# A graph network's edge-maximum passes: the strips' low halves move to VectorE, and every fourth edge block instead of every fifth is fetched by matrix products

## The reference: a four-layer graph network on 3125 nodes and 50000 edges

```
def _sage_pool_layer(x, src, dst, Wp, bp, Ws, Wn, b, n_nodes):
    m = jax.nn.relu(x @ Wp + bp)
    msgs = m[src]
    agg = jax.ops.segment_max(msgs, dst, num_segments=n_nodes)
    agg = jnp.where(jnp.isfinite(agg), agg, 0.0)
    return x @ Ws + agg @ Wn + b
```

```
gathered = support[edge_col] * edge_val[:, None]
out = jax.ops.segment_sum(gathered, edge_row, num_segments=x.shape[0])
```

## Time and profile before

| | us |
|---|---|
| median of 3 timed runs | 2809.11 (2801.65 to 2812.7) |
| the profiled execution, device time | 2804.64 |
| its span, first to last instruction | 2802.9 |
| first pass, window 663 to 1186 | 523 |
| second pass, window 1246 to 1771 | 525 |
| everything before, between and after the passes | 1754.9 |

### The profile page before, as it was taken

How to read it: one execution, slowest core, us unless ns; L and a number is a source line. 1 busy time by engine, 2 the same in 40 slices (tenths; PEclk the granted TensorE clock), 3 DMA queues, 4 the chain that set the end, 5 groups by cost and what they waited for, 6 DMA issues and landing times. The chain is left out here.

```text
span 2802.9 us, 72099 instructions
## 1 busy us (share of the span) xinstructions
PE 2456.9 (88%) x29232; PEld 1982.7 (71%) x29232; DVE 1763.4 (63%) x4833; ACT 1156.4 (41%) x2585; POOL 1299.8 (46%) x1607
## 2 busy tenths in 40 slices
PE   6998999986879888677889887469899999999999
PEld 3666777764556555445556655369899999999998
DVE  6997999986778877446768776320444444444444
ACT  5997888874434444424434444310311111111110
POOL 4007999974888888558888887410000000000000
PEclk8558999997999999789989998569999999999999
DMA  5103000013555555534545555549200000000000
GB/s 165 42 2 102 12 13 13 13 50 97 143 124 141 137 131 135 126 96 122 130 117 150 128 137 143 146 161 348 84 2 2 1 2 2 2 2 2 2 2 19
DMA packets 147170, 227.40 MB, mean 81 GB/s; under 512 B 55568, under 2 KB 112619, under 8 KB 146162
## 3 DMA queue, kind: packets, MB, share of 16 engines
q1 hardware_dynamic: 120350, 184.69, 22.0%
q0 software_dynamic: 22944, 36.72, 6.7%
q10 hardware_dynamic: 3540, 1.30, 0.2%
HBM read 122.26 MB, written 100.35 MB: 79 GB/s over the span
## 5 line engine op out<-in xcount | busy, mean ns | idle before, releaser
L1892 POOL DMA_INDIRECT max_row<-table,max_src_rows x640 | 670.5, 1048 | 181.7 <-issue 165.9
L1934 PE MATMUL max_far<-adj 128*96 128x512 f16 x1800 | 538.6, 401 | 7.7 <-issue 5.8
L2060 DVE TENSOR_SCALAR adj<-adj,node_numbers 128x512 f16<-128x512 f16 x900 | 325.0, 370 | 210.8 <-PE max_far L1934 129.2
L1758 POOL TENSOR_SCALAR e<-e 128x512 f32<-128x512 f32 (+1 forms) x625 | 365.7, 604 | 178.5 <-ACT e L1746 160.9
L2405 PE MATMUL prop<-g,adj 128*128 128x192 f16 x4608 | 387.2, 247 | 8.5 <-DVE g L2479 8.5
L1772 DVE TENSOR_TENSOR e<-e,a_ps 128x1024 f32<-128x1024 f32 (+1 forms) x313 | 372.3, 1195 | 32.6 <-PE a_ps L1684 12.6
L2405 PEld LDWEIGHTS prop<-g,adj 128*128 128x128 f16 x4608 | 380.7, 98 | 13.4 <-issue 9.2
L2405 PE MATMUL prop<-weights_then_states,adj 128*128 128x192 f16 x4608 | 384.3, 246 | 0.0
L2405 PEld LDWEIGHTS prop<-weights_then_states,adj 128*128 128x128 f16 x4608 | 378.9, 98 | 3.7 <-issue 2.5
L1746 ACT ACTIVATE e<-s_ps 128x512 f32<-128x512 f32 (+1 forms) x625 | 335.5, 585 | 60.2 <-PE o_ps L1696 37.8
L2513 DVE SCALAR_TENSOR_TENSOR support_parts<-prop,coef,weights_then_states 128x96 f32<-128x96 f32 x384 | 120.6, 314 | 303.9 <-PE prop L2405 226.0
(11 more groups left out here) (292 smaller groups left out, 3702.5 us busy)
## 6 DMA issues: line engine op xcount, KB each, us to landing
weights_then_states<-weights SPq DMA_DIRECT2D x100, 400.0 KB, 4.8
weights<-max_rows_w SPq DMA_DIRECT2D x52, 400.0 KB
rows_dram<-max_out SPq DMA_DIRECT2D x100, 192.0 KB
weights<-adj SPq DMA_DIRECT2D x48, 400.0 KB
max_same<-same_dram SPq DMA_DIRECT2D x196, 96.0 KB
rows_dram<-adj SPq DMA_DIRECT2D x96, 192.0 KB
max_row<-table,max_src_rows POOLq DMA_INDIRECT x640
adj<-ids_dram SPq DMA_DIRECT2D x36, 128.0 KB
```

Source lines behind the costliest of these rows:

```text
L1758: nc.gpsimd.tensor_scalar(e_tile(u), e_tile(u), math.exp(10.0), math.exp(-10.0), ALU.min, ALU.max).then_inc(clipped, 1)
L1892: nc.gpsimd.indirect_dma_start(row[i % RING][:, j, :], None, table_dram, bass.IndirectOffsetOnAxis(ap=src_rows[:, 4 * n + j:4 * n + j + 1] ...
L1934: mm = nc.tensor.matmul(far_ps[j % 2][0:D, :], parts[:, k, a, :], hot[(T * j + k) % HOTS], start=k == a == 0, stop=k == T - 1 and a == 1)
L2060: nc.vector.tensor_scalar(hot[i % HOTS], ids[j % 2], numbers[:, k:k + 1], None, ALU.is_equal).then_inc(hot_made, 1)
```

## The change

Two things change in `max_pass`, in both passes. The set of far blocks becomes every fourth block instead of every fifth: 22 instead of 18 blocks in a pass, with the first at block 4 instead of 5 and the last at block 88 instead of 90. And the low half of a strip is made by one VectorE instruction, which reads the sum in PSUM and the high half in SBUF and writes their difference. The product `take_high`, its semaphore, and ScalarE's `low_part` are gone. VectorE's new instruction stands right behind the scan in each step.

```
-FAR = range(5, 92, 5)
+FAR = range(4, 92, 4)
...
-            def take_high(n):
-
-                pe.wait_ge(hi_kept, n + 1)
-                nc.tensor.matmul(step_sums(n), minus[:, :], strip_at(0, n),
-                                 start=False, stop=True, skip_group_check=True).then_inc(hi_taken, 1)
...
-                if 1 <= m <= PARTS:
-                    take_high(m - 1)
...
+            def low_part(n):
+                dve.wait_ge(hi_kept, n + 1)
+                nc.vector.tensor_tensor(strip_at(1, n), by_source(n), strip_at(0, n), ALU.subtract).then_inc(lo_kept, 1)
...
                 if m >= SCAN:
                     scan(m - SCAN)
+                if 1 <= m <= PARTS:
+                    low_part(m - 1)
                 far(0, 1)
...
-            def low_part(n):
-                act.wait_ge(hi_taken, n + 1)
-                nc.scalar.activation(strip_at(1, n), by_source(n), ACT.Copy).then_inc(lo_kept, 1)
...
-                if 1 <= m <= PARTS:
-                    low_part(m - 1)
```

More of the change, by code:

```diff
@@ L1841, in max_pass @@
         piece_ps = ctx.enter_context(nc.psum_tensor(f"{name}_piece", [P, 1024], F16))
-        hots_ready, hots_used, hi_kept, hi_taken, lo_kept, piece_turned, piece_kept = (
-            sem("hots_ready"), sem("hots_used"), sem("hi_kept"), sem("hi_taken"), sem("lo_kept"),
+        hots_ready, hots_used, hi_kept, lo_kept, piece_turned, piece_kept = (
+            sem("hots_ready"), sem("hots_used"), sem("hi_kept"), sem("lo_kept"),
             sem("piece_turned"), sem("piece_kept"))
```

## The result

The changed kernel takes 2780.64 us (median of 5 runs, 2774.99 to 2786.23) against 2809.11 before (5 runs). The ratio is 0.9909, 95% interval 0.9890 to 0.9929: 0.9% faster. Its profiled execution took 2784.01 us, against 2804.64. The forecast was 2826 and its range began at 2783; the direction was wrong.

The account below looks back on a forecast made before the run. GpSimd was taken to set the 523 us pass; after the change VectorE's 528 us with 3 of waits gave 531, +8 in each pass, +16 on the profiled 2804.6, so 2826 us timed, range 2783 to 2866.

Parts of the forecast that it names:

- What bounds the kernel: In both passes GpSimd's transfers, issue gaps, first_key and tail sum to the whole 523 us, so GpSimd sets the pace.
- GpSimd's part: 16 fewer transfers save 21.2 us a pass; longer instructions beside a dense VectorE could eat it: 502 to 522 us.
- VectorE's part: Far comparisons add 29.7 us and the subtraction 50, raising VectorE's work from 380 to 459.5 us a pass.
- How full can it get?: VectorE's densest stretches, 0.92 and 0.89, taken as its limit; at 0.89 a pass takes 528 us, at 0.92 512.
- TensorE's part: Far products add 46 us, dropped work takes off 18 and 3; net +25 busy, needing 507 to 527 us a pass.
- The new wait: VectorE's low_part waits for ScalarE's high half of the strip: 3 us a pass, from bounds of 0 and 50.
- The sum: The slowest of three nearly equal engines plus losses between them: 531 us a pass, +8 in each, 2826 us timed.
- Rival 1: The saving survives: VectorE reaches 0.92, GpSimd keeps its durations; 512 us a pass, 2787 us; chance 0.22.
- the rule of the Trainium skill: GpSimd contends with VectorE's two-port or two-SBUF-input instructions; the subtraction, with one PSUM input, would slow no transfer.
- signs listed: If right: VectorE's share 0.87 to 0.90, its TensorE wait well under 67.4 us, subtraction about 0.57, transfers near 1.08 us.
- The one that decides: GpSimd would newly wait for TensorE to free row buffers, 10 us or more a pass against 1.1 before.
- wait of TensorE for far comparisons: This wait of TensorE on VectorE's comparisons was to appear if the forecast was right; no size given.

Follow-up runs that it names:

- e3: Changed kernel with GpSimd's first_key comparing 5 columns of 125 after the first four, output left stale: 2741.12 us, ratio 0.9773 of the kernel before.
- e9: Kernel before with first_key made by ScalarE and every fourth block far, low halves still by TensorE and ScalarE: 2660.10 us, ratio 0.9495.
- e2: Kernel before with only the low halves moved to VectorE's subtraction, every fifth block still far: 2810.42 us, ratio 1.0028.
- e1: Kernel before with only every fourth block far, low halves still by TensorE and ScalarE: 2777.66 us, ratio 0.9912.
- e10: Changed kernel with four buffers for the far comparisons instead of six: 2798.22 us, ratio 0.9983 of the kernel before.
- e4: Changed kernel with every third block far, subtraction on VectorE: 2790.21 us, ratio 0.9960 of the kernel before.
- e5: Changed kernel with first_key made by ScalarE instead of GpSimd, every fourth block far: 2672.15 us, ratio 0.9542 of the kernel before.
- e8: Kernel before with only first_key moved to ScalarE, every fifth block far, low halves by TensorE and ScalarE: 2667.36 us, ratio 0.9515.
- e12: Kernel before with first_key on ScalarE, every fourth block far, even strips' low halves by VectorE, odd by TensorE and ScalarE: 2665.08 us, ratio 0.9501.
- e6: Changed kernel with first_key made by ScalarE and every fifth block far, subtraction on VectorE: 2685.47 us, ratio 0.9589 of the kernel before.

## Why the prediction was wrong, point by point

**What bounds the kernel: right.** GpSimd's sum plus its tail was the pass before and after, and in e3 the pass fell with that sum. The forecast then handed the pass over to the other engines, and that was the error.

**GpSimd's part: right in kind.** The saving of 21.2 us was priced with durations between those of the pass and those of a dense stretch, 502 to 522 us. It came out at 511, in the middle. The longer instructions took 7 us back through the transfers (304 x 0.024) and 5 through `first_key`; a tail of 10.6 us in place of 13.4 gave 3. The text named this term and then let the others override it.

**VectorE's part: the work right, the ceiling wrong.** By the earlier trace rows the subtraction was put at 545 ns for 375 columns and 649 for 475, 571 on the mean; it measured 519 and 625, 546 on the mean. The work was put at 459.5 us and measured 454.9. The first step that failed is "How full can it get?". It read the shares 0.89 and 0.92 in the densest stretches of the earlier trace rows as VectorE's ceiling, and so had a pass of 528 us. In the changed kernel VectorE runs at 0.91 over a whole pass without the tail and at 0.96 between 850 and 950 us, and with every third block far at 0.99. With 0.985 in that formula the pass would have been (459.5 - 2.6)/0.985 + 14 = 478 us, well under GpSimd's 511.

**TensorE's part: wrong too, and by as much.** The text took the 502 us that were left after the wait for fetched rows (523 - 21.3) as TensorE's own need, and came to 507 to 527. That need was never so high. e9 gives TensorE all the work of the changed kernel and `take_high` on top, and its pass takes 450.5 us (at a granted clock of 0.97 against 0.94). The idle time that the trace of before gave to "issue" was counted as TensorE's own. The added work was mis-sized as well: +25 us busy was forecast, +13 measured. The product taken away was near (-18 forecast, -14.5 in e2). The four more far blocks were not: +43 forecast, +27 in e1, where the clock was 0.93 against 0.92. That makes about 0.15 us of busy time for each far product in place of 0.23; why, no run shows. So VectorE's ceiling alone would not have saved the forecast: with 478 for VectorE the largest upper end is TensorE's 527, and the same sum still gives no gain, some 2817 us. Both steps took what an engine does under GpSimd's pace for what it can do.

**The new wait: small, as forecast, but not of the forecast's kind.** 3 us a pass were forecast, as small losses in many steps. The row has 7.2 us, in four waits of 1.6 to 1.9 us, at 695 us and at 1134, 1152 and 1158, and none in the dense middle. It cost no time that shows: e2, with 8.9 us of it, has a pass as long as before (523.1 against 523).

**The sum.** It took the largest of three upper ends and added 3 us, on the ground that three nearly full engines lose time to each other. GpSimd lost 0.2 us to TensorE. That the row buffers between the two took up the rest is likely but not shown. In e10 a shorter ring did cost time, so the thought may have something in it; with six buffers it did not decide.

**The rivals.** Rival 1 (GpSimd keeps its saving, 2787 us) is what happened, within 7 us, at a chance of 0.22. But part of that is luck: it was priced by VectorE at a share of 0.92, 512 us, which happens to fall on GpSimd's own 511; and GpSimd did not keep its durations. By the rule of the Trainium skill beside it, GpSimd would stand near the lower end of 502 to 522 us; it stood in the middle. Of the signs listed, VectorE's share (0.91), its smaller wait (16.3 us) and the transfers (1.070) were near. The one that decides, GpSimd waiting 10 us or more for row buffers, went the other way (0.2 us), and no notable wait of TensorE for far comparisons appeared (2.3 us).

## What to carry to other kernels

When one engine's own instructions and issue gaps add up to the stage and nobody ever stops it, price the change on that engine first, and let another engine take over only when its work exceeds that sum. A busy share seen under that engine's pace is not a ceiling of the others, and the time left after subtracting their visible waits is not their need. Check the pace-maker by cutting its work alone (e3), for a closed sum is no proof where the others are full too (e4). Where a change has two parts, ask of each alone whether it touches the pace-maker: here one did and gained 0.9%, the other did not and gained nothing. Then look at what else stands on the pace-maker and could be made elsewhere: two ScalarE instructions in place of one of GpSimd's were worth four times the change that was studied.

## What the runs showed of the hardware that was not expected

VectorE can be busy for 0.99 of 500 us with waits in its order of work, and TensorE at the same time (e4).

GpSimd's transfers are longer in the midst of a pass than at its end. The last transfers of the first pass, when VectorE has almost nothing left to do, take 0.94 us in the kernel before, the changed kernel, e4, e5 and e9 alike. The mean over a pass went from 1.02 us (e8) to 1.20 (e4, VectorE full). VectorE's busy share alone does not give the figure: outside the tail it is about 0.91 in the changed kernel and in e12, with 1.070 and 1.108 us.

With `first_key` gone from GpSimd a far comparison on VectorE was shorter in all four pairs: 381 to 348 ns (changed kernel, e5), 381 to 358 (e1, e9), 374 to 350 (e2, e6) and 370 to 359 (before, e8). It is not the only cause, since e4, with `first_key` in place, has 358.

A GpSimd comparison of 5 columns takes 693 ns on the mean (100 in a pass, four of them wide), one of 125 columns 867. The medians are 649 and 766 ns, the shortest 327 and 595.
